# Layer 1's mixture of experts: the shared expert over 512 tokens with its weights as the stationary operand, and routed results added into the output in DRAM

## The reference, cut to what matters

```python
x = x + xattn_1(norm(x), ctx)          # 1,024 tokens, 256 features
h = norm(x)                            # rows to the experts
shared = (silu(h @ sg.T) * (h @ su.T)) @ sd.T        # 704 hidden
logits = h @ wr.T + rb                 # 7 routed experts
w, idx = top2(logits), softmax over the two
x = x + shared + sum_c w[c] * expert[idx[c]](h)      # same form as shared
```

## Time and profile before

| | us |
|---|---|
| runs | 664.67, 667.11, 669.02; median 667.11 |
| the profiled execution | 661.33 |
| its span, first to last instruction | 657.0 |
| TensorE busy | 567.2 (86%) |
| VectorE busy | 266.8 (41%) |
| ScalarE busy | 208.5 (32%) |
| GpSimd busy | 56.3 (9%) |
| mean granted TensorE clock | 0.922 of full |

### The profile page before, as it was taken

How to read it: one execution, slowest core, us unless ns; L and a number is a source line. 1 busy time by engine, 2 the same in 40 slices (tenths; PEclk the granted TensorE clock), 3 DMA queues, 4 the chain that set the end, 5 groups by cost and what they waited for, 6 DMA issues and landing times.

```text
span 657.0 us, 8230 instructions
## 1 busy us (share of the span) xinstructions
PE 567.2 (86%) x2953; PEld 375.8 (57%) x2955; DVE 266.8 (41%) x771; ACT 208.5 (32%) x398; POOL 56.3 (9%) x72
## 2 busy tenths in 40 slices
PE   2988899989699997986999899982999999999930
PEld 1545455546688885653454376651666667667620
DVE  5456886722427444845466052511121122222113
ACT  1444445442336444244345521301111111111100
POOL 2200000003020202000000000360000000000035
PEclk9998999967799998787888899997899999999975
DMA  8300019900122312930000160028011100111024
GB/s 308 98 1 1 0 33 354 374 25 32 33 80 65 97 34 87 365 125 2 1 0 1 47 217 1 33 97 274 27 32 33 33 27 25 31 32 33 17 68 142
DMA packets 39618, 53.97 MB, mean 82 GB/s; under 512 B 3789, under 2 KB 30733, under 8 KB 39568
## 3 DMA queue, kind: packets, MB, share of 16 engines
q1 hardware_dynamic: 34272, 44.57, 20.2%
q0 software_dynamic: 2368, 6.32, 3.1%
q10 hardware_dynamic: 2928, 2.44, 1.2%
HBM read 41.11 MB, written 12.20 MB: 81 GB/s over the span
## 4 chain that ended last, share of the span: by engine, by line
PE 68%; issue 14%; DVE 8%; ACT 4%; POOL 2%; SPq 2%; DMA 1%; DVEq 0%; POOLq 0%
PE PS L1498 14%; PE PS L1523 9%; PE PS L674 8%; PE PS L685 7%; PE PS L702 6%; PE PS L1381 4%; PE PS L307 4%; PE PS L1392 4%; PE PS L287 3%; DVE W L819 2%; PE PS L1508 2%; PE PS L276 1%; PE PS L692 1%; ACT W L904 1%; POOL PR L2221 1%
## 5 line engine op out<-in xcount | busy, mean ns | idle before, releaser
L819 DVE TENSOR_REDUCE W<-PS 128x2 f32<-128x512 f32 x128 | 85.6, 687 | 70.2 <-PE PS L674 61.0
L674 PE MATMUL PS<-W 32*128 32x256 f32 x512 | 96.7, 424 | 8.7 <-ACT W L533 6.0
L1498 PE MATMUL PS<-W,PR 128*128 x304 | 97.9, 465 | 0.0
L685 PE MATMUL PS<-W 32*128 32x512 f32 x256 | 93.4, 663 | 3.4 <-ACT W L904 2.7
L674 PEld LDWEIGHTS PS<-W 32*128 32x128 f32 x512 | 63.5, 198 | 43.1 <-issue 18.6
L1523 PE MATMUL PS<-W,PR 128*128 (+1 forms) x324 | 82.1, 396 | 2.8 <-ACT PR L1536 2.2
L1523 PEld LDWEIGHTS PS<-W,PR 128*128 128x128 f32 x324 | 60.4, 194 | 24.4 <-issue 11.4
L1498 PEld LDWEIGHTS PS<-W,PR 128*128 128x128 f32 x304 | 54.8, 190 | 30.3 <-issue 6.0
L1542 DVE COPY PR<-PS 128x128 f32<-128x128 f32 x27 | 7.8, 291 | 109.0 <-PE PS L1508 97.5
L1530 ACT ACTIVATE VR<-PS 128x704 f32<-128x704 f32 x27 | 20.5, 759 | 97.0 <-PE PS L1498 84.7
L1549 DVE TENSOR_TENSOR VR<-VR,PS 128x704 f32<-128x704 f32 x27 | 24.0, 888 | 58.2 <-PE PS L1498 51.5
(11 more groups left out here) (230 smaller groups left out, 640.8 us busy)
## 6 DMA issues: line engine op xcount, KB each, us to landing
W<-in_L_ffn_W SPq DMA_DIRECT2D x16, 512.0 KB, 9.7
W<-in_rgT SPq DMA_DIRECT2D x7, 704.0 KB, 8.2
W<-in_ruT SPq DMA_DIRECT2D x7, 704.0 KB, 9.4
W<-in_rdT SPq DMA_DIRECT2D x7, 640.0 KB, 10.2
W<-in_mask SPq DMA_DIRECT2D x3, 1024.0 KB, 14.0
scratch_x<-W SPq DMA_DIRECT2D x1, 2816.0 KB, 16.2
VR<-scratch_x SPq DMA_DIRECT2D x19, 128.0 KB, 2.1
scratch_y<-VR SPq DMA_DIRECT2D x19, 128.0 KB, 1.7
```

Source lines behind the costliest of these rows:

```text
L674: m = pe.matmul(PS[:, u % 3, q * FK:(q + 1) * FK], QT[r:r + 32, g, c:c + 128], KT[r:r + 32, g, b * FK:(b + 1) * FK], start=True, stop=True)
L685: pe.matmul(PS[:, 3 + u % 3, :], KT[r:r + 32, g, b * FK + kb * 128:b * FK + (kb + 1) * 128], QT[r:r + 32, g, 512 * b:512 * (b + 1)], start ...
L819: dve.tensor_reduce(NM[:, s % 2, q:q + 2, c], PS[:, u % 3, :].rearrange("p (q n) -> p q n", q=2), AX, ALU.max).then_inc(sem("m_free"), 1)
L1498: m = pe.matmul(PS[:, b0 + hf, 0:352], lhs[k], w, start=(k == 0), stop=(k == 1))
```

## The change

`load1` takes the queue as an argument and loads gate and up of a slot in one transfer (the host lays them side by side), so a slot has three transfers. SP loads slots 0 to 5, ScalarE 6 and 7, at the start of its routed program.

The shared expert is done in 12 chunks: for each half of the batch (512 tokens), six blocks of 128 hidden rows, the last one holding 64 rows of gate and 64 of up. A block of the weights is stationary, the 512 tokens move, and the hidden values come out already turned, ready to be the stationary side of the down product, which collects in two banks over the six chunks. The work beside is put after whole chunks, in larger pieces.

For the routed rows there is a table `ws` in DRAM, one pair (token, gate) for each place in the sorted list. It is filled at the start with rows behind the output and gate 0, then by 16 more indirect scatters of 8-byte rows from `whose`. ScalarE loads it as `slots`. The rows with the shared part added are stored to `out` early, by halves; then each routed tile is scaled by its gate as it leaves PSUM and added to `out` by an accumulating indirect transfer from GpSimd, one after another. `out` has 128 rows more, which the host cuts off. The routed program is called inside the arms of `fork` and of the general program instead of after them.

```diff
@@ scratch and constants (pool_start, experts_sp) @@
+        pool.iota(whose[:, :, :, 0].bitcast(I32), pattern=[[0, 2], [128, NT]], base=0, channel_multiplier=1).then_inc(c, 1)
+        pool.iota(nobody[:, 0:1].bitcast(I32), pattern=[[0, 1]], base=NB * S, channel_multiplier=1).then_inc(c, 1)
+        pool.memset(nobody[:, 1:2], 0.0).then_inc(c, 1)
...
+        sp.dma_start(out[NB * S:, :], pad).then_inc(sem("begun"), 16)
+        sp.dma_start(ws.rearrange("(t p) c -> p t c", p=128), nobody[:, :].unsqueeze(1).to_broadcast([128, TILES1, 2])
+                     ).then_inc(sem("wz"), 16)
@@ load1 @@
-        sp.dma_start(up[:, :, 0, :], g.rearrange("(k p) n -> p k n", p=128)).then_inc(sem(f"w_{e}"), 16)
-        sp.dma_start(up[:, :, 1, :], u.rearrange("(k p) n -> p k n", p=128)).then_inc(sem(f"w_{e}"), 16)
+        q.dma_start(up, gu.rearrange("(k p) n -> p k n", p=128)).then_inc(sem(f"w_{e}"), 16)
@@ gates1 @@
-        dve.tensor_tensor(gw[:, 1, :], gw[:, 0, :], rs[:, 4, :], ALU.mult).then_inc(sem("gates1"), 1)
-        dve.wait_ge(sem("gates1"), 1)
+        dve.tensor_copy(whose[:, 0, :, 1], gw[:, 0, :]).then_inc(sem("gates1"), 1)
+        dve.tensor_tensor(whose[:, 1, :, 1], gw[:, 0, :], rs[:, 4, :], ALU.mult).then_inc(sem("gates1"), 1)
@@ the shared expert @@
+    def shared_up(n):
+        b, j = n // NJ1, n % NJ1
+        if n > 1:
+            pe.wait_ge(sem("mul"), n - 1)
+        for w in range(2 if j < NJ1 - 1 else 1):
+            o = w * 640 + 128 * j if j < NJ1 - 1 else 1280
+            for k in range(2):
+                m = pe.matmul(PS[:, 2 * (n % 2) + w, :], W[:, k * 2 * F1 + o:k * 2 * F1 + o + 128],
+                              XT[:, k, 512 * b:512 * b + 512], start=(k == 0), stop=(k == 1))
+            m.then_inc(sem(("up_g", "up_u")[w]), 1)
+
+    def shared_down(n):
+        b, j = n // NJ1, n % NJ1
+        r, o = ROWS1[j], 4 * F1 + j * D
+        pe.wait_ge(sem("mul"), n + 1)
+        if b and j == 0:
+            pe.wait_ge(sem("added"), 2)
+        for t in range(4):
+            m = pe.matmul(half(4 + t // 2, t), HS[0:r, n % 2, t * 128:(t + 1) * 128], W[0:r, o:o + D],
+                          start=(j == 0 and t % 2 == 0), stop=(j == NJ1 - 1), skip_group_check=True)
+        m.then_inc(sem("down1"), 1)
+
+    def shared_pe(beside):
+        pe.wait_ge(*at(1, "w_0", 48))
+        for n in range(CHUNKS):
+            shared_up(n)
+            if n:
+                shared_down(n - 1)
+            beside(n)
+
+    def shared_act(beside):
+        for n in range(CHUNKS):
+            ...
+            act.activation(HS[0:r, n % 2, :], PS[0:r, bank, :], ACT.Silu).then_inc(sem("silu"), 1)
+            if r < 128:
+                act.activation(UC[0:r, :], PS[64:64 + r, bank, :], ACT.Copy).then_inc(sem("silu"), 1)
+            beside(n)
+
+    def shared_dve(beside):
+        for n in range(CHUNKS):
+            ...
+            if b and j < 2:
+                shared_add(0, j)
+            ...
+            dve.tensor_tensor(HS[0:r, n % 2, :], HS[0:r, n % 2, :], up, ALU.mult).then_inc(sem("mul"), 1)
+            beside(n)
@@ beside1 of second_pe @@
-            elif i == 2:
-                pe.wait_ge(*at(1, "rows", 8))
-                for k in range(2):
-                    claim(7, f"rows1_1_{k}")
-                    filled(7, turn4(7, [OB[:, 1, j, :] for j in range(4)], k))
+            elif n == 3:
+                pe.wait_ge(*at(1, "rows", 8))
+                turn_batch("rows1_1", 1)
+            elif n == 4:
+                taken(6, "rows1_1")
                 claim(7, "logits1_1")
                 filled(7, logits_pe(1, 4, 4, 7))
+            elif n == 5:
                 claim(7, "ranks1")
                 filled(7, ranks_pe(2))
@@ beside1 of second_dve @@
+            if n == 0:
+                dve_divide(1, 7, v)
+                add_outputs(v, 1)
+                whole(statistics(v, "rows1_1", rows_of(1)))
+            elif n == 1:
+                dve.wait_ge(*full(7, "logits1_0"))
+                freed(7, logits_dve(1, 0, 4, 7))
+            elif n == 3:
+                dve_xt("rows1_1", 1)
+            elif n == 4:
+                dve.wait_ge(*full(7, "logits1_1"))
+                freed(7, logits_dve(1, 4, 4, 7))
+                dve.wait_ge(*full_free(7, "logits1_1"))
+                whole(choose_experts(v, 2))
+            elif n == 5:
+                dve.wait_ge(*full(7, "ranks1"))
+                whole(places1(v, full_free(7, "ranks1")))
+                whole(tables1(v))
+                gates1(v)
@@ the routed part: pe_way, act_way, dve_way, pool_way, sp_way @@
+            turn_x(0)
+            shared_down(CHUNKS - 1)
...
+            def take_y(r):
+                act.wait_ge(*tile("down1", r + 1))
+                if r == 0:
+                    act.wait_ge(sem("slots"), 16)
+                if r > 1:
+                    act.wait_ge(sem("landed"), 16 * (r - 1))
+                act.activation(YO[:, r % 2, :], PS[:, 6, 0:D], ACT.Identity, scale=slots[:, r, 1:2]).then_inc(sem("y1_out"), 1)
+
+            act.wait_ge(sem("added"), 2)
+            act.dma_start(o_v[:, 0:4, :], X[:, 0:4, :]).then_inc(sem("begun"), 16)
+            act.wait_ge(sem("scattered"), SCATTERED[2])
+            load1(act, 6)
+            load1(act, 7)
+            act_silu(0)
+            act.wait_ge(sem("added"), 4)
+            act.dma_start(o_v[:, 4:8, :], X[:, 4:8, :]).then_inc(sem("begun"), 16)
+            for r in range(1, n):
+                act_silu(r)
+                act_take_h1(r - 1)
+                if r == 1:
+                    act.wait_ge(sem("whose"), 32 * NT)
+                    act.dma_start(slots[:, :, :], ws.rearrange("(t p) c -> p t c", p=128)).then_inc(sem("slots"), 16)
+                take_y(r - 1)
...
+            take_x(0)
+            for h in range(2):
+                shared_add(1, h)
...
+            pool.wait_ge(sem("wz"), 16)
+            pool.wait_ge(sem("gates1"), 2)
+            for c in range(2):
+                for t in range(NT):
+                    off = bass.IndirectOffsetOnAxis(ap=posi[:, c, t:t + 1].bitcast(U32), axis=0)
+                    pool.indirect_dma_start(ws, off, whose[:, c, t, :], None).then_inc(sem("whose"), 16)
+            pool.wait_ge(sem("begun"), 48)
+            pool.wait_ge(sem("slots"), 16)
+            for r in range(n):
+                pool.wait_ge(sem("y1_out"), r + 1)
+                if r:
+                    pool.wait_ge(sem("landed"), 16 * r)
+                off = bass.IndirectOffsetOnAxis(ap=slots[:, r, 0:1].bitcast(U32), axis=0)
+                ins = pool.indirect_dma_start(out, off, YO[:, r % 2, :], None, compute_op=ALU.add)
+                ins.then_inc(sem("landed" if r < n - 1 else "landed_last"), 16)
...
+            sp.wait_ge(sem("scattered"), SCATTERED[2])
+            for r in range(n):
+                load_x(r)
@@ fork, and the end of the program @@
         with e.If(over == 0):
             second()
+            routed(e, i, COUNTS1)
...
-    branch(way[0:1, 0:1], [("tiles", 1), ("gates1", 1)], {w: tiles1(n) for w, n in enumerate(COUNTS1)})
+    sp.wait_ge(sem("begun"), 48)
+    sp.wait_ge(sem("landed"), 16)
+    sp.wait_ge(sem("landed_last"), 16)
```

445 lines of the change are left out of this document (190 added, 255 removed).

## The result

The changed kernel took 614.32 us in the median of four runs (612.07 to 616.20); the kernel before took 668.07 beside it (664.67 to 669.32). The ratio is 0.920, with a 95% interval of 0.915 to 0.925. Two later sets on two different chips gave 618.5 against 662.1 (recorded ratio 0.934, interval 0.926 to 0.941) and 617.7 against 664.0 (0.933, interval 0.927 to 0.940). So the direction is beyond doubt and the size is 44 to 54 us.

The account below looks back on a forecast made before the run. TensorE's array bounds shared expert and routed tiles, order and transfers the gap and tail. Shared -7.5, gap -15.0, stall +10.9, tail -22.8 on a span of 657.0 gave 622.6; median forecast 632.7 us, range 621 to 647.

Parts of the forecast that it names:

- The stall behind the load of the slots: Routed tiles: TensorE's second down waits for the owner and gate table, 8.6 us, plus 2.3 for the low clock.
- between the span and the median: Outside the span: time around it (661.33 - 657.0), plus 5.8 us from the profiled run to the median.
- Columns decide: Shared expert: product time follows columns moved, 37.6 us against 37.5 for up and gate, so no gain there.
- hand-over for each chunk: Shared expert: an allowance of 0.25 us for each of 12 chunks, 3.0 us.
- a stall of 1.6 at the half: Shared expert: the second half's first down waits 1.6 us for VectorE's routing, adds and multiplies.
- The gap: Between shared expert and routed tiles: rows in time and no jump make it shorter, -15.0 us.
- The branch: Gap: with the 19-tile case first inside the first branch's arm, nothing is jumped over; priced 1.0 us, bounds 0 and 4.3.
- 7 us of waiting gone: Gap: weights of slots 6 and 7 move to ScalarE's queue, so SP's row tile lands in time, 2.1 us after issue.
- 2.7 ns a piece: Routed tiles: price per piece of the slots' load, from zeroing the scratch in 1 KB pieces, giving 9.8 us.
- The tail: After the last matmul: gathers, combinations and stores go; evacuation 0.5 and one accumulating scatter 3.5 remain, -22.8 us.
- the first rival: Routed tiles: small pieces cost nearly nothing, slots land by 460, no stall; span 611.7, time 621.8 us; chance 0.17.
- The slower case: Routed tiles: accumulating scatters wait for each other, passing 657 above 9.7 us each; 710 us at 12; chance 0.05.

Follow-up runs that it names:

- second profile of the kernel before: The kernel before, unchanged, profiled once more: 664.75 us, span 660.5.
- the two order experiments: Weights of slots 6 and 7 issued by SP ahead of the first row tile in the changed kernel (638.82 us); behind the first two in the kernel before (654.58).
- the rows first: Kernel before, with SP issuing the weights of slots 6 and 7 behind the first two routed row tiles: 654.58 us against 663.98.
- the probe of the same shape: Changed kernel plus seven SP loads among the routed tiles, 625.88 us in all; this load had 2,816 pieces of 8 bytes.
- slots early: Changed kernel with the table of owners and gates loaded early, unfilled, and the small scatters sent to a second table: 619.81 us.
- scaling later with the weights by SP: Changed kernel with the first two routed tiles scaled in place later, and SP issuing the weights of slots 6 and 7: 619.09 us.
- weights first: Changed kernel with SP issuing the weights of slots 6 and 7 ahead of the first row tile: 638.82 us against 618.5.
- plain scatter: Changed kernel with its nineteen accumulating scatters made plain, the addition left out: 622.42 us against 617.7.

## Why the prediction was too high

Two terms of its sum were mis-sized. The stall behind the load of the slots was put at 8.6 us and 2.3 of low clock, and measured 3.05 and nothing: the load took 3.5 us where the prediction took 9.8. And 10.1 us were put between the span and the median, where the first set had 0.8 (614.3 - 613.5). The first is explained below; the cause of the second is open. With the first alone put right the forecast would have been 624.8, still 10.5 us above the first set's median. The other stretches were 4.2 us shorter (start and shared stage) and 3.0 longer (gap and tail) than predicted, so that most of these errors cancelled.

**Shared expert: the mechanism right, the reserve wrong.** "Columns decide" held: 0.429 and 0.216 us per instruction against 0.427 and 0.213, so no gain in the products, and the 48 transposes are the gain. (The distance of starts in the earlier trace rows is 2.87/12 = 0.239 us with the hand-over, not the 0.213 that the prediction read; the 0.216 bears the price out.) The sum of array and side work was 62.2 us, the stage took 63.2. On top of it the prediction had put 0.25 us of hand-over for each chunk (3.0) and a stall of 1.6 at the half; the timeline has none of the first and 0.19 of the second. With eight up instructions, then eight down instructions of the chunk before, the timeline shows each product ready when TensorE reaches it. The rule for wide moving operands on the page TensorE: Matmul & The Clock Gate (Back-to-back issue gap) of the Trainium skill would have made the up work far cheaper; 0.429 us for 512 columns in a stream of eight disagrees with it for these float32 products of this kernel.

Undoing the part alone gave 7.2 us, near the 7.5 predicted, but that is luck, for two errors cancel. The new stage was predicted at 66.8 us and took 63.2. The old one, cut at the same place as the earlier trace rows and with the slow first product taken off, took 69.6 us in that kernel and 69.6 in the second profile of the kernel before, not the 74.3 from which I had counted (to the last tile's transposes, 70.4 and 71.3). The first profile had waits in it that the others lack, TensorE's timeline of the kernel before:

```profile
440.38 0.88 PE L1508 MATMUL PS<-ident,VR 128*128 128x128 f32 x6 [1.84 <-DVE VR L1549]
...
445.11 3.05 PE L1523 MATMUL PS<-W,PR 128*128 128x256 f32 x12 [1.48 <-ACT PR L1536]
```

I had read this stage as bounded by the array alone, and its last two tiles were not.

**The gap: the size right, -14.0 us of -15.0.** The branch was priced at 1.0 us and cost nothing; undone, it costs 3.0, on ScalarE and VectorE and not on TensorE, where the prediction had looked. The row tile was priced at 2.1 us from its issue and landed 1.56 us late: issued at 432.77, ready at about 438, 5.2 us, in a stretch in which owner scatters and ScalarE's first weights were on the same engines (share 0.98 in 436.45:440.31). The prediction saw the weights only as "7 us of waiting gone"; the two order experiments put 18 to 20 us on that order in the new kernel and 9 to 13 in the old one. Most of the gap before was this order. TensorE's 4.33 us were beside it. SP's 3.34 us were on the way to the row tile and went with the order (0.04 with the rows first), as did 3.5 of another 5.96 us ahead of them, which the prediction did not name.

**The stall: the step that failed in the span.** "22 x 128 = 2,816 pieces of 8 bytes ... 2.7 ns a piece: 7.7 + 2.1 = 9.8 us, which I take." The landing took 3.5 us. The price came from pieces of 1 KB at 375 GB/s, where the bytes set the pace; eight-byte pieces in the same number have 22 KB. The lower bound, 2.1 us for a row tile, was the nearer row. Two errors ahead of it nearly cancelled: GpSimd started its owner scatters 5.5 us earlier than predicted (431.59 against 437.1; its first row scatter was 3.5 us early, at 411.32, and the 2 us for its branch did not appear), but the last of them needed 6.66 us to land where the prediction took 2.1, so that the load went out at 457.22 against 459.5. The stall was 3.05 us, not 8.6, and the clock stayed at 1.00 behind it: 2.3 us more. Together 7.9 us, all but 1.2 of the span's error. The 10.5 ns per packet of the Trainium skill's page DMA: Bandwidth & Descriptors (Measured) would have been, as an estimate, 30 us; the load's 3.5 us disagree, though the probe of the same shape took 23.5 us beside the weights.

**The tail: the size nearly right, -20.8 us of -22.8.** One evacuation and one accumulating scatter were priced at 4.0; they measure 0.47 and 3.8 (609.71 to 613.50), near the 3.5 taken. Missed was what lies between the two: a wait of 1.77 us for the scatter before. "The earlier scatters lie beside tiles of 8.6 us" is true but for the last pair, which is 4.6 us apart (602.87 to 607.47), since no further gate and up stand between the last two downs.

**The chances.** Of the cases, the measured one is nearest to the first rival (slots in time, span 611.7, chance 0.17), with the slots landing at 460.72 where it wanted 460 and a tail 2 us longer. The forecast's mechanism (a stall at the second down, ended by the evacuation behind the slots) was there with a third of its size, and smaller waits beside it (0.16 and 0.43 us). The slower case had its test at d over 9.7 us; the scatters landed in 3.7, 5.34 at most. Even that first rival, 621.8 us as a time, is above all three medians, since it carries the same 10.1 us around the span. And the range was set around a time with 5.8 us of the spread between executions added to it, and in the first set the changed kernel fell on the other side of that spread. On the other two chips its medians (618.5 and 617.7) are below the range too, by 2.5 and 3.3 us.

## What to carry to other kernels

Take the price of a transfer from a row of the same bytes as well as the same pieces, and ask what else is on the engines when it goes: 22 KB in the same pieces took 3.3 to 6.6 us at most places and 23.5 at one. Put the small transfer that the array waits for ahead of the large ones that nobody needs yet; that order alone was worth 9 us in one kernel and 18 to 20 in the other, more than the new tiling. Follow the late transfer back to its issue: in one kernel it was issued late, in the other it travelled long. When a stall goes, look at the granted clock of the next 10 us before booking the gain: in four of the variants (slots early, scaling later with the weights by SP, weights first, plain scatter) 1.7 to 3.3 us were lost there. And price the distance from the span to the median as a term of its own.
